# Second Hadamard stage of a decoder's feed forward: one fp32 product per block, or two one-pass products on a high and a low part

## The chip, the cores and the metric

The kernel runs on one core of one Trainium2 chip, as a single program with five engines that take their instructions in order: TensorE (PE), VectorE (DVE), ScalarE (ACT), GpSimd (POOL) and the engine that issues most DMAs (SP). The time is device microseconds from start to end of one execution. Each kernel was run several times and the median counts.

## The reference, cut to what matters

A decoder layer for 4 batches of 512 tokens with 512 features: a gated recurrent attention, a cross attention, and a feed forward block, each followed by a layer norm. Only the feed forward matters here.

```
gate = bitlinear(x, w_gate);  up = bitlinear(x, w_up)      # x: 2048 tokens x 512, weights 2048 x 512
intermediate = silu(gate) * up                             # 2048 features per token
return h_bitlinear(intermediate, w_down)                   # act_quant(fwht(intermediate)) @ w_down

def fwht(x):     # Walsh-Hadamard transform over the 2048 features, scaled by 1/sqrt(n)
def act_quant(x, bits=8):   # scale by the token's absmax, round, clip; exact to one rounding step
```

The transform of 2048 = 128 x 16 features is a product with a matrix of signs, in two stages: one of 128 x 128 signs, and then one of 16 x 16 signs. The second is done as a 128 x 128 matrix, `np.kron(np.eye(8), bits(16))`, whose entries are 0, 1 and -1.

## The kernel before, in words

The attention runs up to about 1240 us; the cross attention of the last batch still runs beside the start of the feed forward. The order of the feed forward is written out by `ffn_place(n)`: all engines walk the same list of stages for step n, and each engine skips the stages that aren't its own. `n` counts units; a unit is 128 of the 2048 features for the 512 tokens of one batch, so there are 64 units in 16 tiles of four.

In step n, PE does, in this order: `gate` of unit n (eight bf16 products of 512 columns, L639, gate and up), `had2` of unit n - LAG (L654), and `had1` of unit n - 4 (L646 and L648). DVE scales the gate (`gs`, L1198), multiplies in the up part one step later (`h`, L1205, tile M), and takes the absmax of a finished piece (L1209). ACT rounds M into the high part HI (`high`, unit n - 2, L875, type float32r), copies the first stage's result to EV (`had1_out`, L883), copies the second stage's result to H2 (`had2_out`, unit n - LAG - 1, L890), and does the silu of unit n last (L878). POOL forms the low part LO = M - HI (`low`, unit n - 3, L1357). So the first stage already is two products of float32r operands, one with HI and one with LO.

Between the stages the features must be regrouped. SP stores EV to a scratch in memory, and when the 16 units of a batch are there, it reads back 16 x 128 x 128 values per tile into `Z[:, i % 2]` (`read`, 1 MB). `had2` of unit n takes four 128 x 128 blocks of Z as the stationary operands and the sign matrix `C[:, 4, :]` as the moving one, in plain fp32.

Four units make one tile of 128 tokens. A tile then has the stages of the table `TILE`, each a number of steps behind LAG: `scale` (six small DVE instructions, L1221 to L1232), `round` (two on ACT, L897), `clamp` (two on DVE, L1240, tile HQ), `turn_q` (16 transposes on PE, L667), `turn_q_out` (one half of HT by ACT, L903, the other by DVE, L1245), `down` (16 bf16 products of 512 columns on PE, L675), `add` and the statistics of the last norm (L1250 to L1257 on DVE, and then one small power instruction on POOL, L1362), `normal` (L1260) and `store`.

After step 63 no gate is left; PE then has only `had2`, `turn_q` and `down`, for LAG more units. This stretch is called the tail here, and the stretch before it, from the first `down` to the last gate, the steady part. Every instruction waits for counted semaphores; PE takes its eight banks in turn, and each waits until its last reader is done.

Of the kernel before, what the change touches and what calls it, by code (L numbers as in the profile page):

```python
# [8 lines left out]
R = mybir.dt.float32r  # L9
BF = mybir.dt.bfloat16  # L10
ALU = mybir.AluOpType
# [161 lines left out]

LAG = 23


def ffn_place(n):


    for stage, unit in (("gate", n), ("h", n - 1), ("gs", n), ("high", n - 2), ("low", n - 3), ("had2", n - LAG),  # L180
                        ("had1", n - 4), ("had1_out", n - 5), ("had2_out", n - LAG - 1), ("absmax", n - LAG - 2)):
        if 0 <= unit < 64:
            yield stage, unit
# [13 lines left out]
def ffn_order():  # L197
    for n in range(SEAM_UNITS, 60 + LAG + 13):
        yield from ffn_place(n)


FEED = {"gate", "h", "gs", "silu", "high", "low", "had1", "had1_out", "had2", "had2_out", "absmax", "read", "turn_q", "down",
        *(stage for stage, _ in TILE)}
# [12 lines left out]
x_absmax x_limit x_scale x_scaled x_round xq_made xq_turned xt_evac0 xt_evac1 x_spread s_evac idb_made  # L216
gate up gs_made h_silu h_made h_hi h_lo had1 h1_evac z_out0 z_out1 z_in0 z_in1 had2 h2_evac h_absmax h_scale f_made
h_round hq_made hq_turned hq_evac0 hq_evac1 down ffn_add n3_stats n3_aggr n3_var n3_rstd n3_applied
""".split()


def build(nc, x, xT, Wq, Wk, Wv, Wg, Ws, Wo, gw, cT, xWqT, xbq, xWkT, xbk, wgT, wuT, wdT, cst, out):
    with ExitStack() as top:
# [9 lines left out]
        def bank(*use):  # L233
            return banks[at[use]]
# [92 lines left out]
        H2 = sb("H2", [128, 2, 2048])  # L327
        Z = sb("Z", [128, 2, 16, 128])
        M = (M01[:, 0, :], M01[:, 1, :], M2[:])
        XT, SB = (XT0, XT1, XT2), (SB0, SB1, SB2)  # L330
# [79 lines left out]
        def tensor(engine):  # L410
# [218 lines left out]
            def ffn(stage, n):  # L629
# [19 lines left out]
                elif stage == "had2":  # L649
                    i, q = divmod(n, 4)  # L650
                    bh = take(("h2", n), (S["h2_evac"], n + 1))
                    pe.wait_ge(S[f"z_in{i % 2}"], 16 * (i // 2) + 16)
                    for c in range(4):
                        mm = engine.matmul(bh[:, 128 * c:128 * c + 128], Z[:, i % 2, 4 * q + c, :], C[:, 4, :],  # L654
                                           start=True, stop=True)
                    mm.then_inc(S["had2"], 1)
                elif stage in ("turn_q", "down"):
                    ffn_tile(stage, n)
# [48 lines left out]
        def scalar(engine):  # L707
# [162 lines left out]
            def ffn(stage, n):  # L870
# [8 lines left out]
                elif stage == "had1_out":  # L879
                    act.wait_ge(S["had1"], n + 1)  # L880
                    act.wait_ge(S[f"z_out{n % 2}"], 16 * (n // 2))
                    act.wait_ge(S["ov_sum"], 2 * STEPS)
                    engine.activation(EV[:, n % 2, :], bank("h1", n)[:], ACT.Copy).then_inc(S["h1_evac"], 1)  # L883
                elif stage == "had2_out":
                    i, q = divmod(n, 4)
# [55 lines left out]
        def vector(engine):  # L941
# [272 lines left out]
            def ffn_tile(stage, i):  # L1214
# [32 lines left out]
                elif stage == "add":  # L1247
# [4 lines left out]
                    dve.wait_ge(S["ffn_add"], i + 1)  # L1252
                    engine.bn_stats(st3[:, k, :], y).then_inc(S["n3_stats"], 1)
                    dve.wait_ge(S["n3_stats"], i + 1)
                    engine.bn_aggr(mv3[:, k, :], st3[:, k, :]).then_inc(S["n3_aggr"], 1)
                    dve.wait_ge(S["n3_aggr"], i + 1)
                    engine.tensor_scalar(rs3[:, k:k + 1], mv3[:, k, 1:2], EPS, None, ALU.add).then_inc(S["n3_var"], 1)  # L1257
# [47 lines left out]
        def gpsimd(engine):  # L1305
# [46 lines left out]
            def ffn(stage, n):  # L1352
                if stage == "low":
# [3 lines left out]
                    engine.tensor_tensor(LO[:, n % 2, :], M[n % 3], HI[:, n % 3, :],  # L1357
                                         ALU.subtract).then_inc(S["h_lo"], 1)
                elif stage == "add":
                    k = n % 2  # L1360
# [29 lines left out]
        def sync(engine):  # L1390
# [69 lines left out]
            for stage, n in (*seam_order(), *ffn_order()):  # L1460
# [5 lines left out]
                elif stage == "read":  # L1466
# [7 lines left out]
                    for k in range(2):  # L1474
                        sp.wait_ge(S[f"z_out{k}"], 16 * 8 * (b + 1))
                    sp.wait_ge(S["had2"], 4 * n - 4)
                    engine.dma_start(Z[:, n % 2], zs[b].rearrange("a q t -> q a t")[:, :, 128 * i:128 * i + 128]
# [43 lines left out]
```

## Time and profile before

| | us |
|---|---|
| median of 3 runs (1586.12 to 1587.29) | 1586.34 |
| the profiled execution's own time | 1585.25 |
| its span, first to last instruction | 1583.1 |
| PE busy in the span | 1522.7 (96%) |
| DVE / ACT / POOL busy | 1048.2 / 650.9 / 432.4 |
| first and last `had2` | 1337.7 and 1558.8 |
| last gate product | 1500.6 |

Busy shares are means over stages with different limits. The page's slices of 1/40 show DVE mostly at 7 to 8 tenths and ACT at 5 to 7 in the last eight slices but the very last, against mostly 5 to 6 and 3 before; the feed forward is the one stage in which these engines are loaded. PE matmul durations overlap each other, so a group of them is read by the start of the first and the start of what follows.

### The profile page before, as it was taken

The page shows a single profiled execution, that of the slowest core. Times are in us where ns is not written, and L with a number is a line of the kernel's source. Part 1 is how long each engine was busy: PE and PEld are TensorE (multiplying, and loading weights), DVE is VectorE, ACT ScalarE, POOL GpSimd, SP SyncE. Part 2 cuts the span into 40 slices and gives each one's busy share as a digit, 9 for nine tenths or more (in the row PEclk, how much of TensorE's full clock was granted, in tenths as well). Part 3 has the DMA queues.
Part 4 walks back from the last instruction along what each step waited for, and adds up shares of the span by engine and source line. Part 5 has one row for each costly group of instructions (what it writes and reads, how often), then busy time and mean ns, then how long its engine had stood idle before and what let it go on. Part 6 is the DMA issues. An engine that isn't in the chain of part 4 may idle for free.

```text
span 1583.1 us, 24140 instructions
## 1 busy us (share of the span) xinstructions
PE 1522.7 (96%) x9570; PEld 1205.3 (76%) x9570; DVE 1048.2 (66%) x1988; ACT 650.9 (41%) x1245; POOL 432.4 (27%) x282
## 2 busy tenths in 40 slices
PE   6999999999999999999999998989999799999986
PEld 5888888888888888888888887877878656666663
DVE  4556665565556666565556685687677877787885
ACT  4243233333323333343334333333433455776663
POOL 1111011210205544444454222220321144333310
PEclk9999999999999999999999999999999999999999
DMA  7112111121202212222332111101211213444451
GB/s 257 51 53 74 41 47 54 54 67 34 67 1 74 81 67 74 67 67 74 100 98 83 61 41 47 47 8 34 72 43 54 107 59 126 129 142 152 127 167 60
DMA packets 107551, 121.16 MB, mean 77 GB/s; under 512 B 5296, under 2 KB 75056, under 8 KB 107312
## 3 DMA queue, kind: packets, MB, share of 16 engines
q1 hardware_dynamic: 103984, 113.33, 22.7%
q10 hardware_dynamic: 3456, 6.29, 1.0%
q8 instruction: 76, 1.25, 0.3%
q14 instruction: 35, 0.29, 0.1%
HBM read 92.34 MB, written 27.26 MB: 76 GB/s over the span
## 4 chain that ended last, share of the span: by engine, by line
PE 86%; DVE 8%; issue 3%; POOL 1%; DMA 1%; ACT 1%; SPq 0%; POOLq 0%; DVEq 0%; ACTq 0%
PE bank L428 18%; PE bank L430 17%; PE bank L429 17%; PE bank L639 6%; PE bank L675 3%; PE bank L537 3%; PE bank L473 2%; PE bank L654 2%; PE bank L499 2%; PE bank L523 2%; PE bank L482 2%; PE bank L545 2%; PE bank L487 2%; PE bank L494 1%; PE bank L531 1%
## 5 line engine op out<-in xcount | busy, mean ns | idle before, releaser
L428 PE MATMUL bank<-Wh,X 128*128 128x512 f32 x512 | 211.0, 412 | 1.1 <-DVE Y L1076 1.1
L430 PE MATMUL bank<-Wh,X 128*128 128x512 f32 x512 | 200.9, 392 | 0.0
L429 PE MATMUL bank<-Wl,X 128*128 128x512 f32 x512 | 200.0, 391 | 0.0
L428 PE MATMUL bank<-X,Wh 128*128 128x512 f32 x384 | 162.6, 423 | 20.8 <-DVE X L947 12.6
L766 ACT ACTIVATE V<-bank 128x256 f32<-128x256 f32 x128 | 49.0, 383 | 324.5 <-PE bank L430 323.8
L1334 POOL TENSOR_TENSOR sm<-sm,half 128x8 f32<-128x8 f32 x32 | 52.8, 1650 | 388.8 <-DVE sm L1052 388.8
L430 PE MATMUL bank<-X,Wl 128*128 128x512 f32 x384 | 153.1, 399 | 0.0
L1316 POOL TENSOR_TENSOR Wl<-RAW,Wh 128x512 fp32r<-128x512 f32 (+1 forms) x65 | 112.5, 1739 | 146.0 <-ACT Wh L721 146.0
L429 PE MATMUL bank<-X,Wh 128*128 128x512 f32 x384 | 151.8, 395 | 0.0
L639 PE MATMUL bank<-XT,W 128*128 128x512 bf16 x512 | 120.9, 380 | 3.3 <-DVE M L1205 2.5
L1324 POOL TENSOR_SCALAR RAW<-RAW 128x1024 f32<-128x1024 f32 x24 | 87.1, 3629 | 96.9 <-ACT RAW L744 96.9
L428 PEld LDWEIGHTS bank<-Wh,X 128*128 128x128 f32 x512 | 96.3, 188 | 21.0 <-DVE Y L1076 1.3
L430 PEld LDWEIGHTS bank<-Wh,X 128*128 128x128 f32 x512 | 96.1, 188 | 21.2
L429 PEld LDWEIGHTS bank<-Wl,X 128*128 128x128 f32 x512 | 96.6, 189 | 16.7
L995 DVE SCALAR_TENSOR_TENSOR U<-U,bank 128x256 f32<-128x256 f32 x128 | 51.7, 404 | 86.6 <-ACT U L768 86.0
L993 DVE RECIPROCAL ZT<-ZT 128x512 f32<-128x512 f32 x32 | 107.3, 3353 | 1.1
L428 PEld LDWEIGHTS bank<-X,Wh 128*128 128x128 f32 x384 | 73.6, 192 | 44.2 <-DVE X L947 12.5
L1058 DVE SCALAR_TENSOR_TENSOR OG<-bank,sm,U 128x128 f32<-128x128 f32 x256 | 69.1, 343 | 57.3 <-POOL sm L1334 57.3
L1357 POOL TENSOR_TENSOR LO<-M,HI 128x512 fp32r<-128x512 f32 x64 | 81.4, 1281 | 76.0 <-PE bank L648 56.6
L428 PE MATMUL bank<-Woh,OTh 128*128 128x512 f32 x256 | 99.9, 390 | 0.0
L429 PE MATMUL bank<-Wol,OTh 128*128 128x512 f32 x256 | 99.6, 389 | 0.0
L430 PE MATMUL bank<-Woh,OTl 128*128 128x512 f32 x256 | 99.6, 389 | 0.0
(190 smaller groups left out, 3254.6 us busy)
## 6 DMA issues: line engine op xcount, KB each, us to landing
z_scratch<-EV SPq DMA_DIRECT2D x64, 256.0 KB, 2.2
Z<-z_scratch SPq DMA_DIRECT2D x16, 1024.0 KB, 6.0
RAW<-wgT SPq DMA_DIRECT2D x16, 512.0 KB, 3.8
RAW<-wuT SPq DMA_DIRECT2D x16, 512.0 KB, 3.8
RAW<-wdT SPq DMA_DIRECT2D x16, 512.0 KB, 3.6
RAW<-Wo SPq DMA_DIRECT2D x14, 512.0 KB, 3.8
RAW<-Wv SPq DMA_DIRECT2D x26, 256.0 KB, 2.9
RAW<-Wg SPq DMA_DIRECT2D x26, 256.0 KB, 3.3
```

The costliest lines, as they stand in the source:

```text
L428: engine.matmul(o, lh(c), rh(c), start=c == 0, stop=False)
L429: engine.matmul(o, lh(c), rl(c), start=False, stop=False)
L430: last = engine.matmul(o, ll(c), rh(c), start=False, stop=c == n - 1)
L639: mm = engine.matmul(bk[:], w[:, c, 128 * j:128 * j + 128], XT[b % 3][:, c, :], start=c == 0, stop=c == 3)
L766: engine.activation(V[:, par, i, :], bk[:, 0:256], ACT.Copy).then_inc(S["v_evac"], 1)
L993: engine.reciprocal(ZT[:], ZT[:]).then_inc(S["z_recip"], 1)
L995: engine.scalar_tensor_tensor(u, u, 1.0, bank("vg", n, i)[:, 256:512], ALU.add, ALU.mult).then_inc(S["u_made"], 1)
L1058: og = engine.scalar_tensor_tensor(OG[:, h, i, :], bank("o", n, h)[:, 128 * i:128 * i + 128], smv[:, 4, g:g + 1], U[:, par, i, 128 * h:128 ...
L1316: engine.tensor_tensor(lo, r, hi, ALU.subtract).then_inc(S["w_lo_g"], 1)
L1324: engine.tensor_scalar(r, r, MAGIC - 1.0, MAGIC + 1.0, ALU.max, ALU.min).then_inc(S["w3_clip"], 1)
L1334: engine.tensor_tensor(smv[:, 4, :], smv[:, 3, :], half[:, 0:8], ALU.pow).then_inc(S["o_rstd"], 1)
L1357: engine.tensor_tensor(LO[:, n % 2, :], M[n % 3], HI[:, n % 3, :], ALU.subtract).then_inc(S["h_lo"], 1)
```

## The change

The plain fp32 product of the second stage is replaced by two products of float32r operands: `ZH`, the high part of Z, and `ZL = Z - ZH`, both against `K16`, a float32r copy of the signs, which is made once on ACT. Two new stages make the parts, each on two buffers: `zhigh` on ACT two steps before `had2`, and `zlow` on POOL one step before it. LAG goes from 23 to 24, and with it every stage of a tile moves one step back against the gates. The read into Z now waits for `z_lo` where it waited for `had2`. Two semaphores of the last norm are merged into one (`n3_moments`), with the same waits.

```
-LAG = 23
+LAG = 24
-    for stage, unit in (("gate", n), ("h", n - 1), ("gs", n), ("high", n - 2), ("low", n - 3), ("had2", n - LAG),
-                        ("had1", n - 4), ("had1_out", n - 5), ("had2_out", n - LAG - 1), ("absmax", n - LAG - 2)):
+    for stage, unit in (("gate", n), ("h", n - 1), ("gs", n), ("high", n - 2), ("low", n - 3), ("had2", n - LAG),
+                        ("had1", n - 4), ("had1_out", n - 5), ("zhigh", n - LAG + 2), ("zlow", n - LAG + 1), ("had2_out", n - LAG - 1), ("absmax", n - LAG - 2)):
...
+        ZH = sb("ZH", [128, 2, 4, 128], R)
+        ZL = sb("ZL", [128, 2, 4, 128], R)
+        K16 = sb("K16", [128, 128], R)
...
-                    pe.wait_ge(S[f"z_in{i % 2}"], 16 * (i // 2) + 16)
+                    pe.wait_ge(S["idb_made"], 3)
+                    pe.wait_ge(S["z_lo"], n + 1)
                     for c in range(4):
-                        mm = engine.matmul(bh[:, 128 * c:128 * c + 128], Z[:, i % 2, 4 * q + c, :], C[:, 4, :],
-                                           start=True, stop=True)
+                        o = bh[:, 128 * c:128 * c + 128]
+                        engine.matmul(o, ZH[:, n % 2, c, :], K16[:], start=True, stop=False)
+                        mm = engine.matmul(o, ZL[:, n % 2, c, :], K16[:], start=False, stop=True)
...
+                elif stage == "zhigh":
+                    i, q = divmod(n, 4)
+                    if n == 0:
+                        act.wait_ge(S["y_mm"], 4 * STEPS)
+                        act.wait_ge(S["o_lo"], 2 * STEPS)
+                        engine.activation(K16[:], C[:, 4, :], ACT.Copy).then_inc(S["idb_made"], 1)
+                    act.wait_ge(S[f"z_in{i % 2}"], 16 * (i // 2) + 16)
+                    act.wait_ge(S["had2"], n - 1)
+                    engine.activation(ZH[:, n % 2], Z[:, i % 2, 4 * q:4 * q + 4, :], ACT.Copy).then_inc(S["z_hi"], 1)
...
+                elif stage == "zlow":
+                    i, q = divmod(n, 4)
+                    pool.wait_ge(S["z_hi"], n + 1)
+                    pool.wait_ge(S["had2"], n - 1)
+                    engine.tensor_tensor(ZL[:, n % 2], Z[:, i % 2, 4 * q:4 * q + 4, :], ZH[:, n % 2],
+                                         ALU.subtract).then_inc(S["z_lo"], 1)
...
-                    sp.wait_ge(S["had2"], 4 * n - 4)
+                    sp.wait_ge(S["z_lo"], 4 * n - 4)
```

What ACT has in a row in the tail, before; `H<-bank` is `had2_out`, `HT` the first half of `turn_q_out`, `H<-H` the rounding:

```order
L903 ACTIVATE HT<-bank 128x1024 [waits down,hq_turned]
L890 ACTIVATE H<-bank 128x512 [waits had2]
L897 ACTIVATE H<-H,half,fs 128x1024 [waits h_scale]
L897 ACTIVATE H<-H,half,fs 128x1024
L890 ACTIVATE H<-bank 128x512 [waits had2] x2
L890 ACTIVATE H<-bank 128x512 [waits hq_made,had2]
L903 ACTIVATE HT<-bank 128x1024 [waits down,hq_turned]
```

And in the changed kernel, one tile further on in the program:

```order
L897 ACTIVATE ZH<-Z 128x512 [waits had2,z_in1]
L904 ACTIVATE H<-bank 128x512
L911 ACTIVATE H<-H,half,fs 128x1024 [waits h_scale]
L911 ACTIVATE H<-H,half,fs 128x1024
L897 ACTIVATE ZH<-Z 128x512 [waits had2]
L904 ACTIVATE H<-bank 128x512
L897 ACTIVATE ZH<-Z 128x512 [waits had2]
L904 ACTIVATE H<-bank 128x512
L897 ACTIVATE ZH<-Z 128x512 [waits had2]
L904 ACTIVATE H<-bank 128x512 [waits hq_made]
L917 ACTIVATE HT<-bank 128x1024 [waits down,hq_turned]
```

A `ZH` instruction stands before each `had2_out`, and waits for the `had2` of its own step; before the change ACT's copy of HT had only copies of earlier units ahead of it.

What POOL has in a row at the program's end, before; `LO` is the low part of the first stage, `rs` the power instruction of the last norm:

```order
L1362 TENSOR_TENSOR rs<-rs,half 128x1 [waits n3_var]
L1357 TENSOR_TENSOR LO<-M,HI 128x512 [waits had1,h_hi] x4
L1362 TENSOR_TENSOR rs<-rs,half 128x1 [waits n3_var]
L1357 TENSOR_TENSOR LO<-M,HI 128x512 [waits had1,h_hi] x4
L1362 TENSOR_TENSOR rs<-rs,half 128x1 [waits n3_var] x8
L1484 UNCONDITIONAL_BRANCH
```

And in the changed kernel:

```order
L1377 TENSOR_TENSOR ZL<-Z,ZH 128x512 [waits had2,z_hi] x2
L1382 TENSOR_TENSOR rs<-rs,half 128x1 [waits n3_var]
L1377 TENSOR_TENSOR ZL<-Z,ZH 128x512 [waits had2,z_hi] x4
L1382 TENSOR_TENSOR rs<-rs,half 128x1 [waits n3_var]
L1377 TENSOR_TENSOR ZL<-Z,ZH 128x512 [waits had2,z_hi] x4
L1382 TENSOR_TENSOR rs<-rs,half 128x1 [waits n3_var]
L1377 TENSOR_TENSOR ZL<-Z,ZH 128x512 [waits had2,z_hi] x4
L1382 TENSOR_TENSOR rs<-rs,half 128x1 [waits n3_var]
```

In the tail, where POOL had the power instructions alone, four `ZL` instructions now stand between one of them and the next.

## Rows read from the trace of the kernel before

**Rows 1.** The page's part 1: engine, busy us, share, instructions.
```profile
PE 1522.7 (96%) x9570; PEld 1205.3 (76%) x9570; DVE 1048.2 (66%) x1988; ACT 650.9 (41%) x1245; POOL 432.4 (27%) x282
```

**Rows 2.** Windows, columns as headed: two steady periods and a tail period.
```profile
core 0: us, PE busy (x) PEld busy (x) DVE busy (x) ACT busy (x) POOL busy (x), PEclk, DMA share, GB/s
...
1442.30:1459.00 16.70, 16.70 (x105) 10.32 (x105) 13.32 (x27) 11.62 (x20) 5.57 (x5) 1.00 0.34 115
1459.00:1475.70 16.70, 16.70 (x105) 10.35 (x104) 13.31 (x27) 11.60 (x20) 5.59 (x5) 1.00 0.54 166
...
1536.30:1545.40 9.10, 8.12 (x64) 6.12 (x64) 7.47 (x19) 5.50 (x8) 0.54 (x1) 1.00 0.54 144
```

**Rows 3.** Groups by form, 1340 to 1500 us (line, form, count | busy, mean ns).
```profile
L639 PE MATMUL bank<-XT,W 128*128 128x512 bf16 x314 | 74.5, 380 | 1.7 <-DVE M L1205 1.4 <-ACT XT L863 0.2
L1357 POOL TENSOR_TENSOR LO<-M,HI 128x512 fp32r<-128x512 f32 x39 | 49.4, 1277 | 48.7 <-PE bank L648 44.4 <-ACT HI L875 4.3
L654 PE MATMUL bank<-C,Z 128*128 128x128 f32 x312 | 41.2, 275 | 0.2 <-ACT H L890 0.2
...
L875 ACT ACTIVATE HI<-M 128x512 fp32r<-128x512 f32 x39 | 24.2, 620 | 9.1 <-PE bank L648 8.3 <-DVE M L1205 0.8
...
L648 PE MATMUL bank<-LO,H 128*128 128x512 f32 x39 | 15.5, 397 | 0.0
```

**Rows 4.** Instructions of line 560: min/median/max ns.
```profile
L560 PE MATMUL bank<-ws,C x2: 172/212/252, 439.9 to 440.0; 128*128 128x3 f32 x2
```

**Rows 5.** Timeline (start, us, engine), steady period, 1450.5 to 1459.1 us.
```profile
1451.14 0.54 POOL L1362 TENSOR_TENSOR rs<-rs,half 128x1 f32<-128x1 f32 x1 [7.30 <-DVE rs L1257]
...
1451.65 2.51 POOL L1357 TENSOR_TENSOR LO<-M,HI 128x512 fp32r<-128x512 f32 x2
...
1452.82 1.62 DVE L1260 TENSOR_SCALAR Y<-Y,mv,rs 128x512 f32<-128x512 f32 x1
...
1454.54 1.05 PE L654 MATMUL bank<-C,Z 128*128 128x128 f32 x8
```

**Rows 6.** Timeline, one tail period, 1527 to 1546 us.
```profile
1536.29 3.61 PE L675 MATMUL bank<-W,HT 128*128 128x512 bf16 x16 [1.02 <-DVE HT L1245]
...
1539.74 1.95 PE L654 MATMUL bank<-C,Z 128*128 128x128 f32 x16
1539.94 0.75 DVE L1250 SCALAR_TENSOR_TENSOR Y<-bank,fs,Y 128x512 f32<-128x512 f32 x1 [1.26 <-PE bank L675]
...
1540.83 0.60 ACT L890 ACTIVATE H<-bank 128x512 f32<-128x512 f32 x1 [2.40 <-PE bank L654]
...
1541.90 0.54 POOL L1362 TENSOR_TENSOR rs<-rs,half 128x1 f32<-128x1 f32 x1 [8.62 <-DVE rs L1257]
1542.21 1.02 ACT L903 ACTIVATE HT<-bank 128x1024 bf16<-128x1024 bf16 x1
...
1542.41 2.00 PE L654 MATMUL bank<-C,Z 128*128 128x128 f32 x16
...
1544.62 0.68 DVE L1245 COPY HT<-bank 128x1024 bf16<-128x1024 bf16 x1
1544.73 2.37 ACT L897 ACTIVATE H<-H,half,fs 128x1024 f32<-128x1024 f32 x2 [0.57 <-DVE fs L1232]
...
1545.44 0.81 PE L675 MATMUL bank<-W,HT 128*128 128x512 bf16 x3 [1.03 <-DVE HT L1245]
```

**Rows 7.** Timeline at the last batch's read, 1513.9 to 1523.6 us.
```profile
1514.07 0.60 ACT L883 ACTIVATE EV<-bank 128x512 f32<-128x512 f32 x1 [0.27 <-PE bank L648]
...
1523.43 0.35 PE L654 MATMUL bank<-C,Z 128*128 128x128 f32 x1 [2.06 <-DMA Z<-z_scratch]
```

**Rows 8.** Instructions on tile Z: the read's time to landing.
```profile
DMA to landing us min/median/max: 5.5/6.0/7.8
```

**Rows 9.** Windows around an idle PE near the end, columns as in rows 2.
```profile
1560.00:1563.70 3.70, 0.00 (x0) 0.00 (x0) 3.40 (x11) 1.31 (x2) 0.55 (x1) 0.84 0.19 71
1563.70:1570.00 6.30, 6.25 (x17) 2.35 (x18) 1.39 (x2) 1.71 (x2) 0.00 (x0) 0.55 0.00 0
```

More of the change, by code:

```diff
@@ L199, in ffn_order @@
         yield from ffn_place(n)
-FEED = {"gate", "h", "gs", "silu", "high", "low", "had1", "had1_out", "had2", "had2_out", "absmax", "read", "turn_q", "down",
+FEED = {"gate", "h", "gs", "silu", "high", "low", "had1", "had1_out", "had2", "had2_out", "absmax", "zhigh", "zlow", "read", "turn_q", "down",
         *(stage for stage, _ in TILE)}
@@ L216 @@
 x_absmax x_limit x_scale x_scaled x_round xq_made xq_turned xt_evac0 xt_evac1 x_spread s_evac idb_made
-gate up gs_made h_silu h_made h_hi h_lo had1 h1_evac z_out0 z_out1 z_in0 z_in1 had2 h2_evac h_absmax h_scale f_made
-h_round hq_made hq_turned hq_evac0 hq_evac1 down ffn_add n3_stats n3_aggr n3_var n3_rstd n3_applied
+gate up gs_made h_silu h_made h_hi h_lo had1 h1_evac z_hi z_lo z_out0 z_out1 z_in0 z_in1 had2 h2_evac h_absmax h_scale f_made
+h_round hq_made hq_turned hq_evac0 hq_evac1 down ffn_add n3_moments n3_var n3_rstd n3_applied
 """.split()
@@ L1252, in ffn_tile @@
                     dve.wait_ge(S["ffn_add"], i + 1)
[L1253 to L1256, printed above, removed]
+                    engine.bn_stats(st3[:, k, :], y).then_inc(S["n3_moments"], 1)
+                    dve.wait_ge(S["n3_moments"], 2 * i + 1)
+                    engine.bn_aggr(mv3[:, k, :], st3[:, k, :]).then_inc(S["n3_moments"], 1)
+                    dve.wait_ge(S["n3_moments"], 2 * i + 2)
                     engine.tensor_scalar(rs3[:, k:k + 1], mv3[:, k, 1:2], EPS, None, ALU.add).then_inc(S["n3_var"], 1)
```

## The prediction

> **What bounds the kernel now.** I read the page's busy line first: PE is busy for 1522.7 of 1583.1 us [rows 1], so a change pays on PE or not at all, unless it makes PE wait. Next come the windows, because the feed forward has two stretches with different limits. In the steady part a tile of four units takes 16.75 us and PE is busy in all of it, with ACT at 11.6, DVE at 13.3 and POOL at 5.6 us [rows 2]. In the tail a tile takes 1545.44 - 1536.29 = 9.15 us, and PE is busy for only 8.1 of the 9.1 us of a window [rows 2, 6]. There a ring of waits sets the pace: `down` ends, DVE does the add and the statistics, POOL the power instruction, DVE the rest up to its half of HT, and `down` starts again; the last row of the ring names DVE's HT as what PE waited 1.03 us for [rows 6]. So two questions decide: what the new products cost PE where it is full, and what the two new stages add to the ring where it isn't.
>
> **The products.** Each plain product shows as two records (312 records for 39 units of four in the window), and a first-stage float32r product as one (39 for 39 units) [rows 3]. Eight one-pass products per unit therefore mean eight records, as many as before. What does a record cost? Sixteen of them take 1.95 us with a last one of 0.275 [rows 3, 6]: (1.95 - 0.275) / 15 = 0.112 us from start to start, 0.89 us a unit. With a moving operand of only three columns, two records end some 0.11 us apart (172 and 252 ns long, starts 31 ns apart by the trace, so 111 ns) [rows 4]. The record's price is thus mostly not its columns, so it shouldn't fall when the operands are parts. I take 0.112 again: 0 us saved in 64 units. The bounds: above, a one-pass product as dear as a whole plain one, 2 x 0.112, or 57 us more in all; below, half a record, 0.056, which is 0.45 us a unit less, 18 us for the 40 units beside full PE work.
>
> The Trainium skill ("TensorE: Matmul & The Clock Gate", section "Back-to-back issue gap") gives about 81 ns per product for a stream of weight loads and products of 128 columns. The rows here show 112 for fp32 operands [rows 3, 6], and the measurement decides for the old products; by the page's figure, as an estimate, a unit would take 0.65 us, and 40 units would give back some 10 us.
>
> **The new stages in the steady part.** `zhigh` is like L875, 0.62 us, and `zlow` like L1357, 1.28 us [rows 3]. ACT has 11.6 + 4 x 0.62 = 14.1 us of work in 16.75, POOL 5.6 + 4 x 1.28 = 10.7, so both fit. Where they could make PE late is the point after a power instruction: it waits for DVE's variance and ends at 1451.68, then POOL does one `low` and one `zlow`, 2.5 us as the two LO do now, until 1454.2; `had2` starts at 1454.54 [rows 5]. That is 0.3 us of slack. DVE's `normal` now waits for POOL (1.62 us where it takes 0.55 with POOL idle), and there would again be one POOL instruction in its way, not more. ACT's silu comes later, since `zhigh` waits for the step's own `had2`; by my reckoning it is late by less than the slack in three steps of four, and costs about 0.1 us of PE in the fourth. For 8 tiles, and the units before the first `down`, I take 1 us; bounds 0 and 1.2 us per tile (a whole POOL instruction in the way), 10 us.
>
> **The tail, one period.** Count from the first `had2` after a `down`, 1539.74. DVE's add starts at +0.20 and the power instruction ends at +2.70 [rows 6]. POOL is in order, and the `ZL` that the third `had2` needs stands right behind it: it ends at +4.0. Before, that `had2` started at 1542.41, +2.67 [rows 6]; now at +4.05. A reader of its result starts 1.09 us after its start (1540.83 for 1539.74 [rows 6]): +5.15. But this reader is now `zhigh`, and ACT has it, one `had2_out` and its half of HT in a row: 0.62 + 0.5 + 1.02, to +7.3. Before, ACT's half started at 1542.21 and was out of the way by +3.5, and `down` started at +5.70 [rows 6]. So `down` starts 1.6 us later. On its other side ACT goes on with `zhigh`, `had2_out` and the rounding (0.62 + 0.6 + 2.37), after which DVE clamps (0.69) before it may add: 4.3 us less some 0.3 of overlap, against 3.45 us of `down`; the add starts at +0.4, which makes it 1.8 us. Five periods have all of this (from the `down` of tile 8 to that of tile 13; the last units need no further parts): 5 x 1.8 = 9 us. Bounds per period: 0 if the parts were always there in time, and 2.7 (the two instructions' 1.28 and 0.62 with their waits, and nothing overlapped).
>
> **The tail, entering it.** With LAG 24 one `had2` more lies behind the last gate, where PE isn't full: it leaves a place where it cost 0.89 us. In the period in which the gates run out, POOL has `low` and `zlow` behind the power instruction: in the frame of rows 5, 2 x 2.5 us after 1451.68 before the second `had2` can start, where PE now gets there earlier because the gate products are gone. Laid out step by step, I get tile 8's `down` ending 3 us later than now. Bounds: 0 and 5.
>
> **The last batch's read.** EV's last piece is copied at 1514.07 and PE gets its Z at 1523.43, 9.36 us later, after waiting 2.06 us [rows 7]; the read itself takes 6.0 of it [rows 8]. Now it isn't PE that waits first but ACT, two steps earlier in order, and behind it stand `had2_out`, the rounding and, through the clamp, DVE's add. In the frame of the period above the copy starts at +2.1 and Z is there at +11.4; rounding and clamp end at 15.5, the power instruction at 18.0, `zlow` 19.3, `had2`, `zhigh`, `had2_out` and HT at 22.5, when `down` starts. Undisturbed it would start at 10.9 + 7.3 = 18.2. So 4.3 us, less the 1.1 that this place costs already (10.26 us for this period instead of 9.16): 3.2 us. Bounds: 0 and 6.
>
> **The sum**, against the profiled execution's 1585.25: 0 + 1 + 9 + 3 + 3.2 = 16, or 1601.5. That execution is 1.1 us under the median of the runs, so the same sum on the median gives 1602.4; I say 1602. The merged norm semaphore costs nothing: the same DVE instructions wait for the same predecessors. The one copy that makes K16 lies on ACT in step 22, where PE doesn't wait for it.
>
> **Rivals.**
> 1. The tail takes it up. ZH and ZL have two buffers each, and part of the work lies under `down`; if the third `had2` weren't tied to the power instruction, only the steady 1 us and the entering stay: 1587 to 1592. For it: ACT is busy for 5.5 and POOL for 0.5 of 9.1 us [rows 2], so there is room. Against it: the order on POOL puts that `ZL` behind the power instruction. Chance 0.12.
> 2. PE's record falls to 0.056, with the tail's losses as forecast: -18 in the steady part, -0.45 of each tail period (-3), +17 as above: 1582, faster. For it: a float32r product of 512 columns is hardly longer than a bf16 one, 0.40 against 0.38 us [rows 3]. Against it: rows 4. It decides from about 0.065 us a record downward (17 us / 8 records / 46 units below 0.112). Chance 0.06. Between it and the forecast, at the page's figure, 1592.
> 3. The steady part stalls too, because DVE meets POOL twice as often [rows 5], or PE's clock falls in the wait of the last read. After 3.7 us without work (1560.0 to 1563.7) a window has a granted clock of 0.55, nearer the lower of the two levels, and one `down` there takes 6.3 us instead of 3.6 [rows 6, 9]. 10 us for the one, 3 for the other: 1605 to 1615. Chance 0.16.
> 4. One-pass products of 128 columns at the price of whole ones: +57 and more: about 1655. Against it: one record each. Chance 0.03.
>
> **How the numbers follow.** The forecast, with its own range 1596 to 1607, has 0.61; the rest (0.02) is an unforeseen loss or gain. The range of 8 in 10 goes from 1588 (most of rival 1) to 1615 (rival 3). A change under 0.2% (3 us) can't be told from none here. Faster: rival 2 and a little of the rest, 0.08. Same: a third of rival 1, 0.05. Slower: 0.87.
>
> **What would show it.** In the changed profile: L659 and L660 together 512 records, 0.112 us apart, and a steady period of 16.75 to 16.9 us with PE busy throughout. In the tail a period near 10.9 us, where PE's longest wait for L659 is for POOL's ZL behind L1382, and `down` waits for ACT's HT (L917), no longer DVE's. ACT's `zhigh` waiting some 4 us for Z's DMA once, near the last batch's end. The prediction is wrong if the records lie closer than 0.1 us, or if the tail period stays below 9.7 us.

## The result: slower by 45 us, where 16 were forecast

| | before | after |
|---|---|---|
| median, us | 1586.39 (1586.12 to 1587.29) | 1631.43 (1628.49 to 1632.06) |
| ratio, 95% interval | | 1.0282 [1.0269, 1.0295] |
| the profiled execution's own time, and its span | 1585.25, 1583.1 | 1632.06, 1630.3 |
| first gate product to end of the last | 235.9 | 259.0 |
| end of the last gate product to the end | 82.2 | 105.8 |
| first `down` | 1375.27 | 1389.49 |
| steady period | 16.75 | 18.52 |

The direction was right. The forecast of 1602 was too low, and so was the top of its range, 1615. In the profiled executions half of the loss lies in the stretch with gates (23.1 us, forecast about 1), half in the tail (23.6, forecast 15 with the read). The names in the rows below: gate L642, `had1` L649 and L651, `had2` L659 (ZH) and L660 (ZL), `turn_q` L672, `down` L680 on PE; L868 the copy of the turned input XT, `high` L880, silu L883, `had1_out` L888, `zhigh` L897, `had2_out` L904, rounding L911, HT L917 on ACT; absmax L1223, clamp L1254, HT L1259, add L1264, `normal` L1274 on DVE; `low` L1371, `zlow` L1377, the power instruction L1382 on POOL.

**The page's busy line** answers to [rows 1]: as many PE records as before, and 65 more instructions on ACT and 64 on POOL.

```profile
PE 1543.5 (95%) x9570; PEld 1212.8 (74%) x9570; DVE 1055.1 (65%) x1988; ACT 684.0 (42%) x1310; POOL 515.1 (32%) x346
```

**Windows** of two steady periods and of one tail period in which the clock held, for [rows 2]. In the steady part ACT has 13.7 us of work and POOL 10.7, as the prediction added up; but PE is no longer busy throughout, and the period is 1.77 us longer.

```profile
core 0: us, PE busy (x) PEld busy (x) DVE busy (x) ACT busy (x) POOL busy (x), PEclk, DMA share, GB/s
1408.00:1426.52 18.52, 17.05 (x105) 10.36 (x104) 13.47 (x27) 13.73 (x24) 10.71 (x9) 1.00 0.42 129
1426.52:1445.04 18.52, 17.05 (x106) 10.35 (x105) 13.48 (x27) 13.74 (x24) 10.69 (x9) 1.00 0.40 128
...
1575.34:1586.20 10.86, 8.44 (x64) 6.25 (x65) 8.61 (x18) 7.41 (x12) 5.74 (x5) 1.00 0.41 121
```

**Groups by form** from 1390 to 1519 us, for [rows 3]: 112 and 112 records in 28 units, 8 a unit, and the two new instructions with the durations of their models (1280 ns for 1277, 632 for 620). The column at the end is idle time before the group and its releaser.

```profile
L642 PE MATMUL bank<-XT,W 128*128 128x512 bf16 x224 | 53.0, 379 | 10.3 <-ACT H L904 10.3
L1377 POOL TENSOR_TENSOR ZL<-Z,ZH 128x512 fp32r<-128x512 f32 x28 | 35.8, 1280 | 0.0
L659 PE MATMUL bank<-K,ZH 128*128 128x128 f32 x112 | 30.3, 309 | 0.0
L660 PE MATMUL bank<-K,ZL 128*128 128x128 f32 x112 | 26.4, 274 | 0.0
L659 PEld LDWEIGHTS bank<-K,ZH 128*128 128x128 f32 x112 | 21.4, 192 | 3.3
L897 ACT ACTIVATE ZH<-Z 128x512 fp32r<-128x512 f32 x28 | 17.7, 632 | 33.5 <-PE bank L660 32.4 <-DMA Z<-z_scratch 1.0
```

The first row has what the prediction didn't: in the steady part the gate waits 10.3 us in all for ACT's copy of H2, 14 times, so twice a tile. **The timeline** (start, us, engine; in brackets the idle time before and its releaser) shows one of them, where [rows 5] had none:

```profile
1432.45 0.27 PE L660 MATMUL bank<-K,ZL 128*128 128x128 f32 x1
...
1432.76 0.63 ACT L897 ACTIVATE ZH<-Z 128x512 fp32r<-128x512 f32 x1 [1.59 <-PE bank L660]
1432.84 0.40 PE L651 MATMUL bank<-LO,H 128*128 128x512 f32 x1
1433.29 0.58 ACT L904 ACTIVATE H<-bank 128x512 f32<-128x512 f32 x1
...
1434.02 1.89 PE L642 MATMUL bank<-XT,W 128*128 128x512 bf16 x8 [0.78 <-ACT H L904]
```

Read it from the bottom, where PE's gate products (L642) start late. The gate needs a bank, and the bank holds the second stage's result of the unit before. Its copy, L904, has had its data for a whole step, but it stands behind L897 on ACT. L897 refills the ZH buffer that this step's `had2` reads, so it waits for that `had2`, which ends at 1432.72. The bank is free at 1433.9 and the gate starts at 1434.02, 0.78 us late. Two waits of 0.78 and 0.69 a tile are 1.47 of the 1.77 us.

**Ahead of the first `down`** PE also waits 3 us once, for ACT's copy of XT, and then finds its clock at the lower level:

```profile
1371.47 1.01 ACT L868 ACTIVATE XT<-bank 128x1024 bf16<-128x1024 bf16 x1
...
1372.62 3.57 PE L642 MATMUL bank<-XT,W 128*128 128x512 bf16 x8 [3.05 <-ACT XT L868]
```

```profile
1366.00:1372.60 6.60, 2.30 (x14) 1.48 (x13) 2.48 (x4) 4.93 (x7) 2.49 (x2) 0.92 0.11 40
1372.60:1378.00 5.40, 5.38 (x17) 3.35 (x18) 2.49 (x4) 1.54 (x4) 0.00 (x0) 0.50 0.13 49
```

The second window's granted clock is 0.50, which is 1.2 GHz, and the eight gate products take 3.57 us instead of 1.89.

**The tail period in which the clock held**, for [rows 6]:

```profile
1575.34 3.61 PE L680 MATMUL bank<-W,HT 128*128 128x512 bf16 x16 [0.69 <-ACT HT L917]
...
1578.61 0.41 PE L659 MATMUL bank<-K,ZH 128*128 128x128 f32 x1
...
1579.15 0.74 DVE L1264 SCALAR_TENSOR_TENSOR Y<-bank,fs,Y 128x512 f32<-128x512 f32 x1
...
1581.10 0.55 POOL L1382 TENSOR_TENSOR rs<-rs,half 128x1 f32<-128x1 f32 x1 [3.99 <-DVE rs L1271]
...
1581.62 2.68 POOL L1377 TENSOR_TENSOR ZL<-Z,ZH 128x512 fp32r<-128x512 f32 x2
...
1582.93 0.33 PE L659 MATMUL bank<-K,ZH 128*128 128x128 f32 x1 [1.33 <-POOL ZL L1377]
...
1584.08 0.63 ACT L897 ACTIVATE ZH<-Z 128x512 fp32r<-128x512 f32 x1 [2.12 <-PE bank L660]
...
1585.09 1.02 ACT L917 ACTIVATE HT<-bank 128x1024 bf16<-128x1024 bf16 x1
...
1586.21 1.58 PE L680 MATMUL bank<-W,HT 128*128 128x512 bf16 x4 [0.69 <-ACT HT L917]
```

The chain is the forecast one link by link, counted from the first `had2` (1578.61): the third `had2` at +4.32 (forecast +4.05), ACT's part at +5.47 (+5.15), HT done at +7.5 (+7.3), the period 10.86 (forecast near 10.9). But only one period is like that. The seven from the `down` of tile 8 on were 11.90, 14.88, 12.06, 10.86, 12.39, 11.63 and 9.17, after the 17.40 in which the gates run out; before they were 9.15 to 10.26 after 15.22. Twice PE waited about 3 us for ZL: 3.18 us in the period in which the gates run out, and 2.83 us in that of the last read. The clock was lower afterwards:

```profile
1557.34 0.55 POOL L1382 TENSOR_TENSOR rs<-rs,half 128x1 f32<-128x1 f32 x1 [3.99 <-DVE rs L1271]
1557.86 2.67 POOL L1377 TENSOR_TENSOR ZL<-Z,ZH 128x512 fp32r<-128x512 f32 x2
...
1559.17 0.46 PE L659 MATMUL bank<-K,ZH 128*128 128x128 f32 x1 [2.83 <-POOL ZL L1377]
1559.43 0.41 PE L660 MATMUL bank<-K,ZL 128*128 128x128 f32 x1
1559.64 0.41 PE L659 MATMUL bank<-K,ZH 128*128 128x128 f32 x1
```

The records after that wait are 0.213 us apart instead of 0.112, and the `down` behind them, 16 products that take 3.61 us at the full clock, took 4.96. In the tail `down` took 4.74, 5.30, 4.96, 3.61, 5.30, 6.09, 5.30 and 5.30 us, where before all but one (6.36) took 3.6.

A period starts with its `down`, and in the ordinary ones the excess over the forecast is just this: 11.90, 12.06, 10.86 and 12.39, each less what its own `down` took above 3.61, are 10.8, 10.7, 10.9 and 10.7. In these periods PE's longest waits were of 0.7 to 1.3 us only. So the ring is as forecast, and the clock comes on top.

**The last batch's read**, for [rows 7, 8]: ACT waits for the DMA, and POOL for ACT. The time to landing is as before.

```profile
1551.37 0.63 ACT L897 ACTIVATE ZH<-Z 128x512 fp32r<-128x512 f32 x1 [3.06 <-DMA Z<-z_scratch]
1552.08 1.28 POOL L1377 TENSOR_TENSOR ZL<-Z,ZH 128x512 fp32r<-128x512 f32 x1 [3.82 <-ACT ZH L897]
```

```profile
DMA to landing us min/median/max: 5.6/6.0/7.9
```

### The profile page after: what moved, and what is told of

It reads as the page before. It is cut to its first block, busy times and chain, and to the rows that moved or that the text cites. A ratio compares the mean times of both kernels' runs of the same rounds, so it can differ in the third digit from the quotient of the medians.

```text
span 1630.3 us, 24376 instructions
## 1 busy us (share of the span) xinstructions
PE 1543.5 (95%) x9570; PEld 1212.8 (74%) x9570; DVE 1055.1 (65%) x1988; ACT 684.0 (42%) x1310; POOL 515.1 (32%) x346
## 3 DMA queue, kind: packets, MB, share of 16 engines
q8 instruction: 77, 1.26, 0.3%
## 4 chain that ended last, share of the span: by engine, by line
PE 83%; DVE 6%; issue 4%; ACT 2%; POOL 2%; DMA 1%; SPq 0%; POOLq 0%; ACTq 0%; DVEq 0%
PE bank L431 17%; PE bank L433 16%; PE bank L432 16%; PE bank L642 6%; PE bank L540 3%; PE bank L680 3%; PE bank L476 2%; PE bank L502 2%; PE bank L526 2%; PE bank L485 2%; PE bank L548 2%; PE bank L490 1%; PE bank L660 1%; PE bank L497 1%; PE bank L659 1%
## 5 line engine op out<-in xcount | busy, mean ns | idle before, releaser
L642 PE MATMUL bank<-XT,W 128*128 128x512 bf16 x512 | 124.1, 387 | 17.5 <-ACT H L904 11.0
L642 PEld LDWEIGHTS bank<-XT,W 128*128 128x128 bf16 x512 | 47.2, 99 | 82.0 <-issue 24.1
L1371 POOL TENSOR_TENSOR LO<-M,HI 128x512 fp32r<-128x512 f32 x64 | 83.6, 1308 | 56.7 <-PE bank L651 39.2
```

Of the source, the lines that this page charges most:

```text
L642: mm = engine.matmul(bk[:], w[:, c, 128 * j:128 * j + 128], XT[b % 3][:, c, :], start=c == 0, stop=c == 3)
```

## The experiments

Each result is a median with its ratio to runs of the kernel before on the same chip. The kernels ran on different chips, so two of them are compared by their ratios. The last two columns are of the one profiled execution: from the first gate product to the end of the last, and from there to the end. The same code can differ there: b and f are the same program up to the tail, and their first `down` comes 120.9 and 119.1 us after the first gate.

| kernel | us | ratio [95%] | with gates | tail |
|---|---|---|---|---|
| before | | 1 | 235.9 | 82.2 |
| after | 1631.43 | 1.0282 [1.0269, 1.0295] | 259.0 | 105.8 |
| a_out_first | 1612.56 | 1.0171 [1.0154, 1.0188] | 243.7 | 101.3 |
| b_three_bufs | 1611.71 | 1.0166 [1.0150, 1.0181] | 243.5 | 101.7 |
| c_plain_product | 1625.91 | 1.0257 [1.0242, 1.0273] | 257.5 | 100.8 |
| d_lag24_only | 1586.32 | 1.0006 [0.9996, 1.0015] | 236.3 | 82.6 |
| e_three_power_late | 1605.69 | 1.0132 [1.0118, 1.0146] | 243.0 | 98.3 |
| h_bf16_parts | 1603.90 | 1.0115 [1.0101, 1.0129] | 235.0 | 101.0 |
| m_no_tail_parts | 1590.41 | 1.0031 [1.0020, 1.0042] | 239.2 | 82.3 |
| n_steady_parts_only | 1586.58 | 1.0001 [0.9992, 1.0010] | 237.2 | 81.2 |
| o_steady_bf16 | 1580.99 | 0.9966 [0.9953, 0.9979] | 233.1 | 81.3 |

f_three_filler (1606.03), g_before_filler (1583.06) and p_steady_bf16_filler (1578.79) have products put in for the clock, and stand below.

### a_out_first: ACT's copy of H2 ahead of its rounding of Z

```
-  ("zhigh", n - LAG + 2), ("zlow", n - LAG + 1), ("had2_out", n - LAG - 1), ("absmax", ...)
+  ("had2_out", n - LAG - 1), ("zhigh", n - LAG + 2), ("zlow", n - LAG + 1), ("absmax", ...)
```

> The changed kernel with one edit on ACT: had2_out stands before zhigh in each step. Theory (bank chain): PE's gate products wait 0.8 us twice per tile for a bank that had2_out frees, because had2_out stands behind zhigh, which waits for had2 of its own step. Then the steady period falls from 18.52 to 16.8 to 17.0 us and the total by 14 to 18 us, to about 1615; the tail gains under 1 us a tile, since ACT's half of HT is still behind zhigh. Rival (load): ACT and POOL simply have too much work and DVE meets POOL too often; then the order of two instructions changes nothing, 18.3 to 18.5 us and 1628 or more. Rival (products): no change either, 1631.

Measured: the steady period is 16.75 us again, with PE busy in all of it, and the stretch with gates is 15.3 us shorter. The wait in the timeline above was the whole steady loss. Nothing else in the program differs, so the order of two instructions on an engine with 13.7 of 16.75 us of work cost 15 us there. The tail gained 4.5 us as well, where under 1 us a tile was expected.

### b_three_bufs: three buffers instead of two

```
-ZH = sb("ZH", [128, 2, 4, 128], R)      ... act.wait_ge(S["had2"], n - 1)
+ZH = sb("ZH", [128, 3, 4, 128], R)      ... act.wait_ge(S["had2"], n - 2)     # and ZL alike
```

> The changed kernel with three buffers for each of ZH and ZL instead of two, so that zhigh and zlow wait for the had2 of one step earlier; order and work are the same. Bank chain theory: both the wait in the steady part and ACT's half of HT in the tail are freed: steady period 16.8 to 17.0, tail period 10.0 to 10.5 us with PE's clock held (no down longer than 3.7 us), total 1595 to 1603. Rival (load): same instructions, same load, 1625 or more. Rival (products): 1631.

Measured: the same as a_out_first within the intervals, and 9 us above the range that was expected: the steady period is 16.75 us, but the clock did not hold in the tail (four `down`s took 4.8 to 6.5 us). With a third buffer L897 doesn't wait for its own step's `had2`, and L904 behind it is in time. Two different edits that take away the same wait give the same 18 us. Of what is left, 26 us, some 7 lie before the last gate and the rest in the tail. There the wait behind the power instruction is as it was in the changed kernel. Less the excess of their own `down`, the four ordinary tail periods are now 10.1 to 10.4 us, where they were 10.7 to 10.9.

```profile
1543.19 0.55 POOL L1382 TENSOR_TENSOR rs<-rs,half 128x1 f32<-128x1 f32 x1 [3.99 <-DVE rs L1271]
1543.71 3.91 POOL L1377 TENSOR_TENSOR ZL<-Z,ZH 128x512 fp32r<-128x512 f32 x3
...
1545.03 0.48 PE L659 MATMUL bank<-K,ZH 128*128 128x128 f32 x1 [3.02 <-POOL ZL L1377]
```

### c_plain_product: the parts are made, but the product is the old one

```
-  engine.matmul(o, ZH[...], K16[:], start=True, stop=False)
-  mm = engine.matmul(o, ZL[...], K16[:], start=False, stop=True)
+  mm = engine.matmul(..., Z[:, i % 2, 4 * q + c, :], C[:, 4, :], start=True, stop=True)
```

> The changed kernel in which zhigh and zlow still make their parts and had2 still waits for them, but the product is the plain fp32 one from Z and C, as before the change. Bank chain theory: PE's work is the same either way, so 1631 within 3 us, and 0.112 us from record to record in both. Rival (products): the one-pass products are what costs; then 1590 to 1600. If one-pass products were in truth cheaper than plain ones, this would be slower than the changed kernel by more than 3 us.

Measured: 18.62 us for a steady period, like after's 18.52, and 5.5 us less in all. The loss is in making the parts and in what they wait for. That the products themselves became dearer is excluded for the steady part. The gain of 5.5 us (4 by the ratios) lies in the tail (100.8 against 105.8 us), and there PE still waits for ZL as it did. These are the rows of c from 1530 to 1590 us and of after from 1520 to 1603 us (us in total, times, longest):

```profile
PE bank L658 <- POOL ZL L1376: 10.7, 9, 3.1
PE bank L659 <- POOL ZL L1377: 12.0, 10, 3.2
```

What differs is the clock: four of c's eight `down`s took 3.61 us and the eight together 33.5, against one and 40.6 in after. Why the lower clock is met less often with the plain product, after the same waits, is open.

### d_lag24_only: LAG 24 in the kernel before

> The changed kernel without zhigh and zlow and with the plain product: what is left of the change is LAG 24 and the merged norm semaphores. Bank chain theory: 1587 to 1590 (the lag costs one had2 in the tail, and nothing else). Rival (alignment): the lag moves the tile stages against the cross attention of the last batch (PE waited 3.05 us for ACT's copy of XT there, with its clock at half afterwards); then 1595 or more.

The edit is the one number, with the merged semaphore; no part is made. Measured: no difference in time. The first `down` is 3 us later, the tail's first period shorter (13.37 against 15.22).

### e_three_power_late: as b, with POOL's power instruction one step later

```
-                elif stage == "add":        # POOL's place for the power instruction
+                elif stage == "normal":
```

> Three buffers for the parts, and POOL does the power instruction of the last norm one step later, so that the ZL which the third had2 of a tile needs no longer stands behind it. The theory for the tail: PE waits there for POOL's ZL (3.0 us at most in the run with three buffers), because that ZL stands behind an instruction that waits for DVE's variance; then its clock falls and the down takes 4.7 to 6 us. If so, the tail period falls from 11 to 12.8 to 9.2 to 10 us, every down from tile 8 to 13 takes 3.6 us, and the total is 1595 to 1600. Rival (DVE): DVE's own chain is what bounds the tail, and normal, which now comes later, makes it longer: tail periods stay at 10.5 or more, total 1606 or more.

Measured: 5 to 6 us less than b, above the 1595 to 1600 expected. PE waits for ZL less (5.6 us in all, 13.0 in b), but tail periods are 10.1 to 13.0 up to tile 13, and `down` still took up to 6.5 us. So the tie of ZL to the power instruction explains a part only, and the rival (DVE's own chain) has the larger one. What PE waited for longest is now DVE's half of HT:

```profile
PE bank L680 <- DVE HT L1259: 13.3, 7, 3.8
PE bank L659 <- POOL ZL L1377: 5.6, 7, 1.6
```

(us in total, times, longest.) In that chain L1274, DVE's `normal`, takes 1.48 us when a ZL runs on POOL beside it, and 0.55 when none does. Before, POOL was idle there; so even with the best order the period would be some 9.15 + 0.93 = 10.1 us. Less the excess of their `down`, three of e's periods are that, and three of b's four ordinary ones were so already.

### f_three_filler and g_before_filler: is it the clock?

```
+                    if n >= 41 and n % 4 == 1:      # f: as b, ahead of had2, its result overwritten
+                        for c in range(6): engine.matmul(bh[:], WG[:, c % 4, 0:128], XT[0][:, c % 4, :], ...)
```

```
+                    if i >= 14:                     # g: the kernel before, ahead of the last two downs
+                        for c in range(12): engine.matmul(bk[:], WG[:, c % 4, 0:128], XT[0][:, c % 4, :], ...)
```

> Three buffers for the parts, and in the tail six products of 512 columns whose result nobody reads stand on PE ahead of the wait of every third had2 of a tile (1.3 us of PE work in a wait of up to 3 us); order and waits of all else as with three buffers. If the fall of PE's clock is a cost of its own beside the wait, the downs of tiles 8 to 13 all take 3.6 us and the total falls by 5 to 9 us against three buffers (1611.7), to 1603 to 1607. If the wait alone counts, the total is the same or up to 2 us more.

> The kernel before the change, with twelve products of 512 columns whose result nobody reads on PE ahead of the waits of the last two downs (2.6 us each, in waits of 3.7 and 3.0 us). In the trace of the kernel before, the down of tile 14 takes 6.36 us after an idle stretch of 3.7 us, the others 3.6. If the idle stretch is what lowers the clock, this down takes 3.6 us too and the total falls by 2 to 2.8 us, to about 1583.7; if not, 1586.4 or more.

Measured: f takes 1606.03 us (1.0130), 5.7 us under b by the ratios, though PE does more: the last periods are 10.09, 10.08, 9.15 and 9.16. The expectation held in the total and not in its condition: the `down`s of tiles 8 and 10 still took 5.5 and 5.8 us. Of the distance between the two profiled executions (6.3 us), only 2.9 us lie behind the last gate, where the products were put in; the rest lies where the two programs are the same. g takes 1583.06 (0.9985 [0.9976, 0.9994]), 2.3 us under before. Its row stands against the 6.3 us `down` of before, at a clock of 0.55 [rows 9]:

```profile
1560.75 2.75 PE L673 MATMUL bank<-XT,W 128*128 128x512 bf16 x12
1564.67 3.61 PE L678 MATMUL bank<-W,HT 128*128 128x512 bf16 x16 [1.17 <-DVE HT L1248]
```

The twelve products (of 512 columns) are the first row. PE waits for the same DVE instruction, but for 1.17 us and not 3.76, and its clock is still at the upper level when the work comes. So the lower clock is a cost of its own beside the wait. How much of after's loss it is follows from the rows above: the eight `down`s of its tail took 11.7 us more than at the full clock, those of before 2.8. Outside the period of the last read, which waits for the DMA, it is 10.0 against 2.8, or some 7 us of the tail's 23.6. No run with the clock held throughout confirms this sum.

### h_bf16_parts: as e, with ZH, ZL and K16 in bf16

Two bf16 parts keep some 16 bits of the value.

> As the run with three buffers and the later power instruction, but ZH, ZL and K16 are bfloat16 instead of float32r, which changes the result a little: high and low part together keep 16 bits of each value. Its PE records should then start 56 ns apart like the bf16 transposes of the kernel before, not 112: 0.45 us a unit instead of 0.89. If PE bounds the steady part alone, its period falls by 1.8 us, to 14.95, and the total by 13 to 18 us against the float32r run. If the chain over ACT, DVE and POOL is close behind, the steady period falls to 16 us or so only, and the total by 4 to 8 us. If the record's price weren't set by the weight load, nothing changes.

Measured: 1603.90 us, 2 to 3 us under e where 13 to 18, or 4 to 8 in the second case, were expected. The records are now 0.056 us apart, and the steady period is 15.49 us (one of seven took 19.01, when PE waited for DVE and ACT for Z). A unit's eight records take 0.45 us instead of 0.90, four units 1.8; of these 1.26 show. The stretch with gates is 8 us shorter than e's, and the tail 2.7 us longer: its `down`s took up to 6.6 us. Rival 2's price exists, then, but bf16 has it and float32r hasn't. Both operands changed their type here, so which of them sets the price is not shown. The window of one period, and the groups of the products from 1390 to 1430 us:

```profile
1444.21:1459.70 15.49, 15.48 (x105) 8.44 (x104) 12.47 (x27) 13.18 (x23) 10.63 (x9) 1.00 0.45 147
```

```profile
L659 PE MATMUL bank<-K,ZH 128*128 128x128 bf16 x44 | 6.1, 219 | 0.0
L660 PE MATMUL bank<-K,ZL 128*128 128x128 bf16 x44 | 6.1, 219 | 0.0
L660 PEld LDWEIGHTS bank<-K,ZL 128*128 128x128 bf16 x44 | 4.3, 98 | 1.3
```

### m_no_tail_parts and n_steady_parts_only: where the remaining 26 us are

```
+PARTS = range(0, 40)      # n: range(12, 40); as b, but other units take the plain product and make no parts
```

> Three buffers as in b_three_bufs, but only units 0 to 39 take the two one-pass products on parts; units 40 to 63, whose second stage lies after the last gates, take the plain product again and the order of the tail is that of before with LAG 24. Theory (the loss of b_three_bufs, 26 us, is the stretch before the first down plus the parts in the tail, nothing else): steady period 16.75, tail periods 9.15 as before and first down at 1387, so 9 to 11 us over the kernel before: 1594 to 1597. Rival (the tail's loss comes from LAG 24, the read or the length of the queues): tail periods stay above 10 and the time stays near 1610.

> As m_no_tail_parts, but units 0 to 11, before the first down, take the plain product too, so the parts are made for units 12 to 39 only. Theory: nothing of the loss is left, since float32r products cost what the plain ones do and the parts are hidden in the steady part: 1585 to 1588, the steady period 16.75, first down at 1378. Rival (a smaller steady loss was hidden under the others, such as DVE's normal beside POOL): 1589 to 1595.

Measured: without parts in the tail the tail is 82.3 us, as before, and each period but the first and the last 9.15: of b's 26 us, 21 go by the ratios, 19.4 of them in the tail by the profiles. The first `down` comes 2 us later after the first gate than in n (116.6 against 114.7 us); that, and a `down` at the lower clock of 6.34 us against n's 5.30, is 3 us of m's 4 to 5 over n. The profiles show no more behind the first gate product. The expectation of 9 to 11 us for the stretch before the first `down` was too high: in b nearly the same code took 4 us more there than in m, with PE waiting 3.0 us for XT instead of 1.7. In that stretch the two differ in what the reads wait for (`z_lo` in b, `had2` in m). That this is the cause was not tested, and c speaks against it for the wait: its reads wait for `had2` too, and PE waits 3.05 us for XT as in after. Nearly 2 us can be scatter, as b and f show. n is level with before: float32r parts for 28 units, ACT at 13.6 and POOL at 10.7 us of 16.75, cost nothing and bring nothing.

```profile
1408.00:1424.75 16.75, 16.75 (x106) 10.37 (x105) 13.37 (x27) 13.63 (x24) 10.68 (x11) 1.00 0.47 143
```

### o_steady_bf16 and p_steady_bf16_filler: parts only where PE is full

```
 PARTS = range(12, 40)
-ZH = sb("ZH", [128, 3, 4, 128], R)
+ZH = sb("ZH", [128, 3, 4, 128], BF)     # ZL and K16 alike; p: with g's twelve products
```

> As n_steady_parts_only, with ZH, ZL and K16 in bf16 for those 28 units, which keeps some 16 bits of the value instead of float32's 24. A record costs 0.056 instead of 0.112 us there (h_bf16_parts), 0.45 us a unit, on the 28 units at most 12.6 us. Theory (PE's work is the bound in the steady part): steady period 15.0 to 15.5 while the parts are in it, 1574 to 1579, faster than before. Rival (ACT and POOL, or DVE's normal beside POOL, take the place of PE in the shorter period): periods of 16 and more, 1580 to 1586.

> As o_steady_bf16, with 12 idle-filling bf16 products of 128 columns ahead of the last two downs, as in g_before_filler, which gained 2.3 us. Their result is overwritten. Theory (the two gains add, the one in the steady part and the other by the clock at the end): 2 to 3 us under o_steady_bf16, 1572 to 1577. Rival (the shorter steady part changes what PE waits for at the end): equal to o_steady_bf16 within 0.1%.

Measured: o gains 5.4 us, about half of what it was expected to. Its steady period is 16.16 us and its time 1580.99, both within the rival's ranges and outside the theory's. PE no longer is busy throughout; `had1` comes to wait for DVE's M a little in nearly every tile:

```profile
1441.98 0.22 PE L667 MATMUL bank<-K,ZL 128*128 128x128 bf16 x1
1442.38 0.50 PE L650 MATMUL bank<-HI,H 128*128 128x512 f32 x1 [0.18 <-DVE M L1226]
```

All such waits are 0.28 us a period, of the 0.67 between 16.16 and h's 15.49; the rest is not explained. h had the power instruction one step later; whether o would gain by that was not run. The twelve products of p have 512 columns, as in g, not 128. p takes 1578.79 us (0.9954 [0.9941, 0.9966]), 2.2 under o. The intervals of the two overlap, but the traces agree: the `down` of tile 14 takes 3.61 us where it took 5.30 in o, and the gap to the next is 1.7 us shorter. So the gains seem to add, though p stayed above its expected 1572 to 1577. It is the fastest kernel of this study, some 7 us under the one before, at the price of 16 bits in 28 of 64 units.

## Why the prediction was wrong, by its own steps

**The products, 0 us: the number right, the argument in part lucky.** 512 records, 0.112 us apart. Rows 4 said that a record's price is mostly not its columns, and that holds. But from this the prediction went on to "it shouldn't fall when the operands are parts", and by the same argument bf16 parts would have saved nothing either; they cost half (0.056 us, h). So the type decides, which rows 4 could not tell. The weight load of a float32r block shows as 0.192 us, like that of a plain fp32 one, and that of a bf16 one as 0.098. Which of the load and the product is the one that paces a pair, no run separates.
The Trainium skill ("TensorE: Matmul & The Clock Gate", "Back-to-back issue gap") has 81 ns for loads and products of 128 columns. Neither type here has it. The Trainium skill ("TensorE: Matmul & The Clock Gate", "Weight-path perf modes") also says that a faster weight load is on for 128 weights of a type other than FP32. The durations of the loads agree for fp32 and bf16, with float32r on fp32's side.

**The new stages in the steady part, 1 us: this step failed.** The prediction checked POOL against the `had2` that needs the parts, and found 0.3 us of slack; that was right. Of ACT it said that the silu comes later because `zhigh` waits for the step's own `had2`, "late by less than the slack in three steps of four", 0.1 us in the fourth. It followed the wrong successor. Behind `zhigh` on ACT stands `had2_out` first, as the list of ACT's instructions in the changed kernel shows, and that instruction frees a PSUM bank for the gate. Its lateness cost 1.77 us in every steady period, of which 1.47 show as waits of the gate, and 15 us in all with the units before (a_out_first, b_three_bufs). The bound of 1.2 us a tile was a POOL instruction's length; it did not bound a wait of another engine. Rival 3 had the steady part stall, but by DVE meeting POOL, and priced at 10 us for a different cause.

**The units before the first `down`, under the same 1 us: undersized.** No row of that stretch was read. After takes 124.0 us from the first gate to the first `down`, b, without the bank wait, 120.9, m 116.6, n 114.7, and LAG 24 alone (d) 113.7. So about 10 us were lost there, 3 by the bank wait and 7 otherwise. ACT still copies the turned input there, and PE's longest wait was for that copy; why it comes late is not shown.

**The tail's period, 9 us for five: mechanism right, the clock left out.** 10.86 us where the clock held, forecast near 10.9, and 10.7 to 10.9 in the other ordinary periods less the excess of their `down`. These `down`s took 1.1 to 2.5 us more than at the full clock, also those of tiles 13 to 15, behind the five periods that were counted. The forecast had the clock only in rival 3, for one wait. Together the tail lost 23.6 us where 9 + 3 + 3.2 were forecast. The 8.4 missing are some 7 for the clock, by the sum under g_before_filler, and 2 for entering the tail, less 1 by which the rest came out under its forecast.

**The last read, 3.2: near. Entering the tail, 3: too small.** The read's period was 14.88 us, against a forecast of 10.9 + 4.3 = 15.2. From the end of the last gate product to the end of tile 8's `down` it was 16.8 us, against 10.4 before: 6.4 us more, where 3 were forecast. Of these, 1.3 come with LAG 24 alone (d), 4.0 with the parts, and 1.1 are the clock.

**A slip in rival 4.** 57 us on top of 1602 are 1659, not 1655; nothing hangs on it.

**The check lines.** "A steady period of 16.75 to 16.9 us with PE busy throughout" was the one that the trace refuted; the others (512 records, the wait for ZL behind L1382, `down` waiting for ACT's HT, ACT waiting some 4 us for Z once, here 3.06) came true. Of these, `down` waited for ACT's HT at tiles 9, 11 and 12 only, and the tail period near 10.9 us stood in the trace once.

The loss of 45 us, by ratios on 1586.4: the bank wait behind `zhigh` 18 (after to a or b), parts in the tail 21 (b to m), parts before the first `down` 5 (m to n), float32r products and parts in the steady part 0 (n to before). Each of the differences has an uncertainty of 2 to 3.5 us, and the middle two are less cleanly parted than the names say: by the profiles 19 us of b to m lie in the tail, and 2 of m to n before the first `down`.

## What to carry to other kernels

An instruction that is put into an engine's order delays whatever stands behind it: list all of those, and for each ask what it frees, a PSUM bank above all, not only what it computes. Room by busy time (13.7 of 16.75 us) says nothing of this. Splitting an fp32 product into float32r parts paid nothing here, at 128 columns; bf16 parts did. And look where the idle engines' new work falls: the parts cost nothing in the stretch where PE is full, and some 20 us in the tail, where a ring of waits sets the pace. Last, price the lower clock wherever a change adds waits to PE.

## What the runs showed of the hardware that was not expected

- A float32r product of 128 columns with a weight load of its own costs what one record of a plain fp32 product does, 0.112 us; a bf16 one 0.056.
- After waits of 2.8 to 3.8 us TensorE's granted clock was mostly at the lower level, and the `down` behind them took 4.7 to 6.5 us for 3.61. The length of the wait alone doesn't tell: before's last one, 2.98 us, left the next `down` at 3.61, and in the changed kernel `down` took up to 6.09 us where the waits before it were 0.7 to 1.3 us. Twelve products ahead of each of the last two `down`s, 2.75 us a group, gained 2.3 us on a kernel that was otherwise left alone.
- A DVE instruction of 0.55 us takes 1.48 us beside a POOL tensor operation (in before too, 1.62 [rows 5]), and this made e's ring some 0.9 us longer, though that DVE instruction doesn't read the ZL that POOL makes meanwhile.
